# A decoder layer in one program: shared block 0 begun in the attention's last steps, two pairs of weight stages, the way down three slices behind, high parts on ScalarE

## What is computed

```
x = x + linear_attention(layernorm(x))            # elu features, no heads
x = x + cross_attention(layernorm(x), ctx)        # 77 context rows, softmax
x = x + ffn(layernorm(x))                         # shared expert + 2 of 8 experts
ffn(z) = gelu(z @ Wfc_s + bfc_s) @ Wproj_s + bproj_s
       + sum over the two best experts e of gate_e * (gelu(z @ Wfc[e] + bfc[e]) @ Wproj[e] + bproj[e])
```

## Time and profile before

| | us |
|---|---|
| median of 3 runs | 805.7 (804.74 to 807.33) |
| profiled execution | 812.28 |
| its span, first to last instruction | 810.6 |
| TensorE busy | 752.4 (93%) |
| VectorE busy | 616.2 (76%) |
| ScalarE busy | 383.3 (47%) |
| GpSimd busy | 227.8 (28%) |
| mean granted clock of TensorE | 0.97 |

### The profile page before, as it was taken

The page is one execution under the profiler, slowest core; times in us unless marked ns, Lnnn a source line. Parts: engine busy times, 40 slices in busy tenths (PEclk is TensorE's granted clock), DMA queues, the critical chain, the costliest instruction groups (busy, mean ns, idle before and its releaser), DMA issues.

```text
span 810.6 us, 21882 instructions
## 1 busy us (share of the span) xinstructions
PE 752.4 (93%) x6919; PEld 622.3 (77%) x6919; DVE 616.2 (76%) x1870; ACT 383.3 (47%) x865; POOL 227.8 (28%) x221
## 2 busy tenths in 40 slices
PE   3899999999639999999999999999999999999995
PEld 1677777777428788877878888888888889887783
DVE  4689999998669997877886667667666677777774
ACT  4657666765215544444453333333333334555552
POOL 3210111011100015555521333333333333333333
PEclk9999999999659999999999999999999999999998
DMA  6466787755332458777762444454544444355451
GB/s 204 147 155 171 193 209 176 180 133 94 83 108 86 139 158 239 224 230 222 230 191 60 67 65 64 67 65 65 67 68 67 68 65 63 66 74 71 70 70 25
DMA packets 163123, 97.29 MB, mean 120 GB/s; under 512 B 105260, under 2 KB 158408, under 8 KB 163016
## 3 DMA queue, kind: packets, MB, share of 16 engines
q1 hardware_dynamic: 149720, 78.81, 40.8%
q0 software_dynamic: 13296, 17.09, 12.8%
HBM read 38.73 MB, written 36.15 MB: 92 GB/s over the span
## 4 chain that ended last, share of the span: by engine, by line
PE 79%; DVE 9%; issue 3%; DMA 3%; ACT 2%; SPq 1%; POOL 0%; DVEq 0%; ACTq 0%
PE bank_kv L1361 8%; PE bank_kv L1362 7%; PE bank_kv L1363 7%; PE bank L1340 5%; PE bank_st L1340 5%; PE bank_st L1338 5%; PE bank_st L1339 5%; PE bank L1339 5%; PE bank L1338 5%; PE bank_kv L1354 4%; PE bank_kv L1259 4%; PE bank_st L1244 3%; PE bank_st L1212 3%; PE bank_kv L1355 2%; PE bank L1266 2%
## 5 line engine op out<-in xcount | busy, mean ns | idle before, releaser
L1361 PE MATMUL bank_kv<-w_parts,expert_buffers 128*128 (+1 forms) x656 | 179.5, 274 | 8.7 <-DVE expert_buffers L1132 7.9
L771 ACT ACTIVATE expert_buffers<-bank_st,bias_columns 128x256 f32<-128x256 f32 (+1 forms) x248 | 108.2, 438 | 157.9 <-PE bank_st L1340 111.8
L771 ACT ACTIVATE expert_buffers<-bank,bias_columns 128x256 f32<-128x256 f32 (+1 forms) x248 | 108.2, 438 | 152.2 <-PE bank L1340 76.4
L1363 PE MATMUL bank_kv<-w_parts,expert_buffers 128*128 (+1 forms) x656 | 179.1, 273 | 0.0
L1362 PE MATMUL bank_kv<-w_parts,expert_buffers 128*128 (+1 forms) x656 | 179.1, 273 | 0.0
L1131 DVE TENSOR_SCALAR expert_buffers<-expert_buffers 128x256 f16<-128x256 f32 x328 | 103.2, 315 | 82.6 <-ACT expert_buffers L771 72.1
L1132 DVE SCALAR_TENSOR_TENSOR expert_buffers<-expert_buffers 128x256 f16<-128x256 f32 x328 | 139.6, 426 | 11.3
L613 POOL DMA_INDIRECT out<-expert_buffers,token x71 | 117.9, 1661 | 18.1 <-issue 16.9
L594 POOL DMA_INDIRECT rows_by_expert<-rows,dest_rows x64 | 66.2, 1034 | 109.1 <-ACT expert_buffers L771 93.4
L1338 PE MATMUL bank_st<-expert_buffers,w_parts 128*128 128x256 f16 (+1 forms) x368 | 86.9, 248 | 1.1 <-DMA expert_buffers<-rows_by_expert 1.1
L1340 PE MATMUL bank<-expert_buffers,w_parts 128*128 128x256 f16 (+1 forms) x368 | 87.0, 248 | 0.0
(11 more groups left out here) (198 smaller groups left out, 1543.8 us busy)
## 6 DMA issues: line engine op xcount, KB each, us to landing
rows_by_expert<-w_parts SPq DMA_DIRECT2D x12, 795.0 KB, 5.3
stage_w<-in_L_ffn_Wfc SPq DMA_DIRECT2D x16, 512.0 KB
stage_w<-in_L_ffn_Wproj SPq DMA_DIRECT2D x16, 512.0 KB
expert_buffers<-in_L_ffn_bproj SPq DMA_DIRECT2D x46, 128.0 KB
rows<-in_x SPq DMA_DIRECT2D x16, 256.0 KB, 5.0
x_residual<-rows SPq DMA_DIRECT2D x16, 256.0 KB, 2.4
expert_buffers<-x_residual SPq DMA_DIRECT2D x16, 256.0 KB
out<-expert_buffers SPq DMA_DIRECT2D x16, 256.0 KB
```

Of the source, the lines that this page charges most:

```text
L771: act.activation(spare[:, at], hid[c % 4][:, 0:width(G)], ACT.Gelu_apprx_tanh, bias=bias, scale=UNSCALE).then_inc(s["gelu_done"], 1)
L1361: pe.matmul(y, g[:, 0, tile(t)], w_hi, start=f == 0 and t == 0, stop=False, skip_group_check=True)
L1363: op = pe.matmul(y, g[:, 1, tile(t)], w_hi, start=False, stop=f == FC - 1, skip_group_check=True)
```

## The change

It has six parts that hang together.

1. *The attention's end.* `step` runs to i = 17 only. Scores, softmax and transposes of batch 15 follow by themselves; then the stream of blocks begins. The products with batch 15's values stand behind up(1), batch 14's logits behind slice 3, batch 15's behind slice 9. On VectorE and ScalarE the third norm of batch 15 stands in slices 1 and 2. `top_two` is cut in eight pieces for all batches together, in slices 10 to 17. The counts stand at slice 19, `route(3)` is the first routing part at slice 21 and `route(19)` stands at slice 40.
2. *The way down* is three slices behind in shared blocks, and the evacuation comes at f = 3 instead of 2. The first routed block goes back to two.
3. *Conversions* begin at slice 28, one half every 6 slices (the last at slice 120): ScalarE at the second and fourth slice of the six, VectorE's four pieces at the third to sixth.
4. *Two pairs of stages*: halves 1, 3, ... 13 go through the region of halves 14 and 15 of `w1`, so a half may be loaded while the one before is being converted.
5. *High parts on ScalarE* (a Copy with scale 16) for slices 0 to 27 and every odd slice after.
6. *The gates' exponential* is a power on GpSimd instead of an Exp on ScalarE.

```diff
-TOP_STEPS = {19: range(0, 15), 20: range(15, 16)}
+CONVERT_FROM, CONVERT_EVERY = 28, 6
+TOP_SLOT, COUNT_SLOT, ROUTE_SLOT = 10, 19, 21
+ROUTE_ORDER = (3, 4, 5, 6, 7, 8, 0, 1, 2, 9, 10, 11, 12, 13, 14, 15, 16, 17, 18, 19)
...
+        lent_stage = [words(w1, 2 * E - 2 + c, 1) for c in range(2)]
...
-        LAG_FULL, LAG_HALF = 2, 6
+        LAG_SHARED, LAG_FULL, LAG_HALF = 3, 2, 6
+        def split_by_act(c):
+            return c < FC * NSH and (c < CONVERT_FROM or c % 2 == 1)
+        def converting(c, at):
+            if c - at == FC * (NSH - 1):
+                return NSH - 1
+            half = (c - at - CONVERT_FROM) // CONVERT_EVERY
+            if (c - at - CONVERT_FROM) % CONVERT_EVERY == 0 and 0 <= half < NSH - 1:
+                return half
+            return None
+        def in_lent(half):
+            return half < NSH - 2 and half % 2 == 1
...
 # SP
-            for i in range(-2, B + LAG + 1):
+            for i in range(-2, LAST + 3):
                 step(i)
-            sp.wait_ge(s["logits_done"], B)
-            sp.wait_ge(s["pads_stored"], PAD_STEPS * 16)
+            load_half(0, 2)
+            turn_third(LAST - 1)
+            store_x2(LAST)
...
-            for G in range(NSH - 1):
-                load_half(G, G + 2)
-                shared_block(G, G % 2)
+            shared_block(0, 0)
+            turn_third(LAST)
+            sp.wait_ge(s["logits_done"], B)
+            sp.wait_ge(s["pads_stored"], PAD_STEPS * 16)
+            load_half(1, 2)
+            for c in range(FC, FC * NSH - 2):
+                if (half := converting(c, -5)) is not None and 1 < half < NSH - 1:
+                    load_half(half, half + 1)
+                if c % FC == 4 and c < FC * (NSH - 1):
+                    shared_block(c // FC, c // FC % 2)
 # GpSimd
+            pool.wait_ge(s["route_step"], 1)
+            pool.tensor_tensor(edlog, base_e, dlog, ALU.pow).then_inc(s["exp_gate"], 1)
 # ScalarE, in a slice behind the gelu
+                    if split_by_act(c):
+                        if c >= 4:
+                            act.wait_ge(s["down_done"], c - 3)
+                        got(act, "gelu_done", c)
+                        act.activation(gs[f % 4][:, 0, :], spare[:, :], ACT.Copy, scale=A_SCALE)\
+                            .then_inc(s["g_hi_act"], 1)
+                    if (half := converting(c, 2)) is not None:
+                        convert_last(half, w1, stage_of(half)[0], "w1_", "w1_hi")
+                    if (half := converting(c, 4)) is not None:
+                        convert_last(half, w2, stage_of(half)[1], "w2_", "w2_hi")
+                    if c == 2:
+                        high_third(LAST)
 # VectorE, in a slice behind the low part
-                    if G < 5 and f < 4:
-                        route(4 * G + f)
-                    if f == (2 if G < FIRST_HALF else 5) and G > 0:
+                    if c == 1:
+                        dve.wait_ge(s["rstd_ready"], LAST + 6)
+                        layer_norm(2, LAST)
+                    elif c == 2:
+                        low_third(LAST)
+                    elif TOP_SLOT <= c < TOP_SLOT + 8:
+                        top_two(c - TOP_SLOT)
+                    elif ROUTE_SLOT <= c < ROUTE_SLOT + len(ROUTE_ORDER):
+                        route(ROUTE_ORDER[c - ROUTE_SLOT])
+                    if f == (3 if G <= NSH else 2 if G < FIRST_HALF else 5) and G > 0:
 # TensorE
-                lag = LAG_FULL if G < FIRST_HALF else LAG_HALF
+                lag = LAG_SHARED if G < NSH else LAG_FULL if G < FIRST_HALF else LAG_HALF
...
+                    if c == 1:
+                        weigh_values(LAST)
+                    elif c == 3:
+                        route_logits(LAST - 1)
+                    elif c == 9:
+                        route_logits(LAST)
+                    elif c == COUNT_SLOT:
```

More of the change, by code:

```diff
@@ L409, in load_half @@
                 c = w2_shared[half - 2 * E] if shared else w2_half[ds(half, 1)].rearrange("a p c n -> p (a c) n")
+                at, name = flat_stage, "loaded"
+                if not shared and in_lent(half):
+                    at, name = lent_stage, "lent"
                 sp.wait_ge(s["w1_lo"], before)
-                sp.dma_start(stage1[:, :], a).then_inc(s["w1_loaded"], 16)
+                sp.dma_start(at[0], a).then_inc(s["w1_" + name], 16)
                 sp.wait_ge(s["w2_lo"], before)
-                sp.dma_start(stage2[:, :, :], c).then_inc(s["w2_loaded"], 16)
+                sp.dma_start(at[1].rearrange("p (c n) -> p c n", c=4), c).then_inc(s["w2_" + name], 16)
             def turn_norm(n, b):
@@ L733, in _, with convert_last @@
                     .then_inc(s["proj_hi"], 1)
-            for i in range(-2, B + LAG + 1):
+            for i in range(-2, LAST + 3):
                 step(i)
-            act.wait_ge(s["route_step"], 1)
-            act.activation(edlog, dlog, ACT.Exp).then_inc(s["exp_gate"], 1)
-            def convert_last(half, w, stage, loaded, done):
-                act.wait_ge(s[loaded], (HALVES - 2 * E + half + 1) * 16)
+            exp_scores(LAST)
+            high_third(LAST - 1)
+            copy_prob(LAST)
+            def convert_last(half, w, stage, name, done):
+                act.wait_ge(s[name + ("lent" if in_lent(half) else "loaded")], stage_loads(half) * 16)
+                if w is w1 and half == NSH - 2:
+                    act.wait_ge(s["w1_lo"], HALVES - 2 * E + half)
+                elif w is w1 and half == NSH - 1:
+                    act.wait_ge(s["w2_lo"], HALVES - 2 * E + half - 1)
                 act.activation(w[:, half * 2048:half * 2048 + 1024], stage, ACT.Copy, scale=W_SCALE).then_inc(s[done], 1)
```

324 lines of the change are left out of this document (181 added, 143 removed).

## The result

The changed kernel takes 794.35 us (790.67 to 795.7, four runs), the kernel before 805.22 beside it: a ratio of 0.9864 [0.9843, 0.9885], 10.9 us less. The forecast was 783.4 with 22.3 us less, and a range of 777 to 793. The sign was right, half of the gain is missing, and the time lies 1.35 us above the range. The profiled execution took 793.37 us for a span of 791.6, against 812.28 and 810.6 before: in the profiles the gain is 19 us, in the timed runs 11. That gap is the larger part of the story: the 812.28 us of before lie outside its timed runs (803.93 to 807.33), while the 793.37 us of after are one of its timed runs.

What follows compares the result with a forecast made beforehand. VectorE was taken to pace the shared stage, TensorE the routed blocks. 224.9 + 165.3 + 3.2 + 1.3 + 1.5 + 2.7 + 2.5 = 401.4, plus 0.7 is 402.1 against 424.4: 22.3 off 805.7 gives 783.4 us, range 777 to 793.

Steps and rivals of the forecast that it cites:

- The step that failed: Shared stage: VectorE paces it where conversions and evacuations bunch up, losing 14.1 us over 15 blocks, 2.7 after the change.
- The second half of the same step: Baseline: the saving of 22.3 us, read from the 812.28 us profile, was subtracted from the timed median of 805.7.
- Start: Start of the shared stage: up(0) follows the attention's last transposes directly, at 224.9 us instead of 237.54.
- the wait at down(0): First way down: TensorE waits 1.5 us for slice 0's low part, behind batch 15's context and variance on VectorE.
- the clock's rise: Start of the shared stage: TensorE's clock rises 4.5 us after 224.9, at about 229.4; 1.3 us lost before.
- Copies on ScalarE: Shared stage: 78 of 128 high parts move, up to 34 us less on VectorE, at 0.45 us each on ScalarE.
- The routing's slices: Slices 31 to 40: VectorE falls 5.2 us behind, so TensorE waits 2.7 us, bounds 0 and 5.
- End of the stage: Before the first routed slice: evacuating one slice later raises TensorE's wait from 1.1 to 2.5 us.
- today's chain of 8.1 us: Stage's end, kernel before: from gelu(122) at 416.18 to the landed transpose at 424.27; forecast 8.4 after the change.
- A: Rival, shared stage: the hand-over still paces it, 12 of the 14.1 us stay, 792.7 us; chance 0.16.
- B: Rival, after slice 16: GpSimd's power stops VectorE for up to 7.1 us, 788.0 us; chance 0.07.
- C: Rival, shared stage: weight loads come late and ScalarE waits, slower than before, 828 us past 13.5 us landing; chance 0.04.

Runs made afterwards that it cites:

- e13: Kernel before, unchanged, profiled again in a slower session: 810.83 us, ratio 0.9996, blocks 5 to 14 in 113.52 us.
- e14: Kernel before without GpSimd's 64 indirect sends of rows, in the session of e13: 802.69 us, ratio to before 0.9897.
- e15: Changed kernel, unchanged, run again in the session of e13: 801.19 us, ratio to before 0.9865.
- e7: Kernel before with only the high part of every second slice moved to ScalarE: 809.66 us, ratio to before 0.9966.
- e1: Kernel before, unchanged, profiled again: 804.68 us, profile 804.38, ratio 1.0001.
- e9: Kernel before, unchanged, profiled once more in a faster session: 804.24 us, ratio 0.9999, blocks 5 to 14 in 107.00 us.
- e2: Changed kernel, unchanged, run again in the session of e1: 794.19 us, ratio to before 0.9876.
- e3: Changed kernel with the first routed block's transposed load ahead of shared block 15's loads on SP's queue: 788.18 us, ratio to before 0.9798.
- e11: The same kernel as e3, repeated in the session of e9: 789.18 us, ratio to before 0.9795.
- e4: Changed kernel with batch 15's products, both batches' logits and batch 15's third norm back ahead of the stream: 803.85 us, ratio to before 0.9983.
- e5: Changed kernel with all high parts of the shared blocks back on VectorE: 802.83 us, ratio to before 0.9885.
- e8: e3 with the high parts of all slices below 44, instead of 28, on ScalarE: 796.26 us, ratio to before 0.9801.
- e12: The same kernel as e8, repeated in the session of e9: 788.53 us, ratio to before 0.9791.
- e17: Kernel before with its 64 scattered sends replaced by plain copies of the same rows into another tensor: 805.17 us, ratio to before 0.9934.
- e6: Changed kernel with the way down two slices behind in shared blocks, as before: 804.99 us, ratio to before 0.992.

## Why the prediction was half right

**The step that failed** is the first one: "VectorE paces the shared stage, and only where conversions and evacuations bunch up", with its 14.1 us over 15 blocks, of which I kept 2.7. In blocks 5 to 14 it does not hold. The earlier trace rows name L1132 for 7.9 us of TensorE's waits, and the earlier trace rows show a slice of 1.38 us; both are true, but VectorE there was the last link of a chain that began with late counts of TensorE, on which ScalarE's gelu waited, beside the scattered sends (e13, e14). Without the sends these blocks take 104.80 us with all of VectorE's work left in place. The change leaves these sends as they are, and so their cost: from up(0) to up(128) it takes 187.4 us in e15 against 187.6 in e13, nothing less, where I had forecast 10.4 less. In A sessions, where the sends cost little, it is 178.4 against 180.5 to 180.9. In blocks 1 to 4 the step does hold (e7).

**The second half of the same step** is the baseline. I saw that the profile lay 6.6 us above the timed median, wrote "no row says where those went, so I take the difference over unchanged", and subtracted a saving that included them. e1 and e13 show where they went: blocks 5 to 14, 113.7 against 106.7 us. By these blocks the profile that I read was of kind B (e13 repeats it), while the timed runs, near 805 us, were of kind A: I took a saving read in one kind off a time of the other. Rows do say it, but only beside a second profile. Against e1's up(128), 416.32, my own forecast of 401.4 would have given 14.9 less 0.7, or 14.2 us; the timed runs gave 10.9.

**Start.** Forecast 12.6 us, measured 11.7 (up(0) in e1 and e9 at 235.85, in e2, e3 and e11 at 224.1 on average); e4 gives 9.7 by the medians. The order in time, the low clock, the wait at down(0) (1.17 for 1.5) and the clock's rise (229.6 for 229.4) came as worked out.

**Copies on ScalarE.** Taken at 0.45 us, measured 0.416 (78 of them). VectorE is busy 25.5 us less, not 34: I priced a high part by the 0.44 of the earlier trace rows, but alone it takes 0.29 and the next operation begins after 0.33; the row I took was a long one.

**The routing's slices.** Forecast 2.7 us with 5 as the upper bound. Blocks 1 to 14 take 150.1 us where TensorE needs 146.3: 3.8 lost, inside the bounds. I had forecast one gap near slices 35 to 43; blocks 2, 3 and 4 take 11.3, 13.3 and 11.3 us, so the loss lies in slices 19 to 43, most of it in 27 to 35. Block 3, from one L1200 to the next:

```profile
267.33:280.66 13.33, 12.82 (x117) 11.01 (x116) 12.71 (x35) 8.75 (x17) 0.00 (x0) 1.00 0.32 91
```

VectorE, the third busy figure, works 12.71 of 13.33 us. The cause was right here, the place some slices too late.

**End of the stage.** Forecast 2.5 us of wait, measured 3.4, with the clock's fall behind it another 1.6 us that I had not counted. I took over today's chain of 8.1 us and never asked what in it could go. e3 shows that the wait hangs on order: three transfers on SP stand ahead of the one that TensorE waits for.

**Summed up against the profile before**, up(128) came 21.3 us earlier (forecast 23.0) and the rest of the span takes 2.4 us longer (forecast 0.7), 18.9 in all against 22.3. That leaves 3.4 us for the changed kernel and 8 for the baseline. The nearness is luck in part: the profile of after has blocks 5 to 14 at 104.64 us as a session of kind A has them; in B (e15) they take 114.48 and the span is 800.1 us, 8.5 more.

**Rivals.** A (the hand-over still paces the stage, 792.7) came nearest in time, for another reason: only 2.2 us of waits for L1235 besides the one at down(0). Its mechanism is not what kept the time up. B falls. GpSimd's power, in order of time, and VectorE's low parts beside it:

```profile
253.20 5.59 POOL L643 TENSOR_TENSOR w_parts<-w_parts 128x32 f32<-128x32 f32 x1 [11.03 <-DVE w_parts L919]
```

```profile
254.03 0.42 DVE L1235 SCALAR_TENSOR_TENSOR expert_buffers<-expert_buffers 128x256 f16<-128x256 f32 x1
254.90 0.43 DVE L1235 SCALAR_TENSOR_TENSOR expert_buffers<-expert_buffers 128x256 f16<-128x256 f32 x1 [0.46 <-ACT expert_buffers L845]
```

It takes 5.59 us, inside 1.3 to 7.1, and two low parts run in it at their usual 0.42. The Trainium skill ("SBUF — State Buffer", section "SBUF: two separate sides") has a VectorE operation with two SBUF inputs and a GpSimd operation that reads SBUF hold a shared port pair by turns, each for a whole instruction; by that rule the first of these would have ended only behind 258.8. This trace does not agree for the power, as it did not before (L955). C falls: ScalarE waited 0.4 us in all for a weight half. The load on the DMA engines was forecast at 280 GB/s and 0.94 over the stretch; it came out lower, but rose to 1.00 and above for 10 us at a time, and still no half came late by more than these 0.4 us (columns as in the earlier trace rows):

```profile
300.00:400.00 100.00, 99.67 (x914) 89.09 (x911) 83.00 (x194) 71.87 (x139) 55.03 (x56) 1.00 0.81 266
310.00:320.00 10.00, 10.00 (x94) 8.97 (x92) 8.71 (x22) 7.48 (x15) 6.07 (x7) 1.00 1.01 363
340.00:350.00 10.00, 10.00 (x94) 8.96 (x93) 8.86 (x21) 6.86 (x14) 6.54 (x7) 1.00 1.02 351
370.00:380.00 10.00, 10.00 (x94) 8.97 (x93) 8.93 (x22) 7.36 (x15) 6.03 (x6) 1.00 1.00 334
```

**The range.** Both its ends were savings taken off 805.7, and nothing in it stood for the 6.6 us that no row explained. Had the saving been allowed to shrink by them, 790 would have been as near as 783, and 793 no upper end.

## What to carry to other kernels

When the profiled execution lies further from the timed runs than these scatter, take a second profile and subtract stretch by stretch before pricing anything: the gap sat in the very stretch that I was pricing. A wait names the last link; an engine is the pace only if it is busy all through the stretch. Where a producer ahead of it rests, look for what ended the rest, and whether that came when it should. Where several transfers stand in one queue, order them by who waits soonest: here one moved line gave 6.0 us by the medians in A and 3.5 in B; between the profiles of e2 and e3 it is 4.9, of which up(128) comes 2.2 us sooner after up(0) and the clock behind it gives 2.6.

## What the runs showed of the hardware

- The same kernel has two times that hold through a session: 804.6 and 811.4 to 811.9 us. Nearly all of the difference (6.5 of the 6.9 us between the spans of e9 and e13) lies in the 100 us with scattered sends, where ScalarE rests up to 3.3 us at a time (14 times over 1.3 us in e13, 8 in e15), at fixed places of the program. Without the sends both kinds give 104.80 us for the ten blocks. What makes a session one or the other is open: it is not simply the chip, since the records give the same chip number for e5 to e8 (811.92) and e9 to e12 (804.63).
- What ScalarE waits for in these rests is, in 12 of the 14 of e13, TensorE's count of finished ways up, which rises late; in the example it rose 2.5 us after the last matmul's start instead of 0.29. Why TensorE's counts come late beside the sends in B, and not in A, is open. It is neither bytes nor DMA load (e17).
- A wait of 3.4 us on TensorE, which had been busy up to it, was followed by a fall to 1.2 GHz (clock 0.50 and 0.69 in the two stretches behind it); behind waits of 0.9 us (e3) and 2.1 us (e6) the clock stayed at 1.00.
